# Two attention layers and their dense stages on one core: first tiles loaded a stage ahead, four row copies instead of eight, and a planned order with new costs

## The chip, the cores and the metric

The kernel runs on one core of one Trainium2 chip. The metric is device microseconds from start to end of one execution. The core has five instruction queues: TensorE (PE), VectorE (DVE), ScalarE (ACT), GpSimd (POOL) and SyncE (SP), which here only issues DMAs. Each takes its instructions strictly in the order in which they were written; they meet through semaphores.

## The reference, cut to what matters

```python
x = x + attn_a(layernorm(x))     # 2 x 2048 tokens, 256 wide, 16 heads of 16, causal
x = x + ffn(layernorm(x))        # 256 -> 1024 -> 256, gelu, weights replaced by alpha * sign(w)
x = x + attn_b(layernorm(x))     # biases, output projection, layernorm of its own with gamma, beta
x = x + ffn(layernorm(x))        # the same weights

def attn_a(x):
    q, k, v = heads(x @ W_attn)
    att = softmax(where(causal, q @ k.T / 4, -inf))
    att = att * decay            # after the softmax: falls with the distance, 0 from 511 tokens on
    return merge(att @ v) @ W_proj
```

All is float32. attn_b is the same without the decay, with biases and a normalisation behind its projection.

## The kernel before, in words

Six stages follow one another with a barrier of all engines between them; each has tiles and semaphores of its own, and tensors go from stage to stage through DRAM. They are `setup` (signs of the feed-forward weights), `projections` ("qkv_a": normalise x, q, k and v), `attention` ("att_a"), `dense` ("mid": output projection, residual, feed-forward, then q, k and v of the second attention), `attention` ("att_b") and `dense` ("end").

**Attention.** Tokens go in chunks of 512 (c = 0 to 3), heads in groups of 4; with two sequences that makes 8 groups (g = 0 to 7). A group's work has two halves. *Maxima* ("M"): PE multiplies 128 queries by up to 512 keys (line 982) and VectorE reduces that to the rows' negative maxima (lines 910 and 914); there are 160 a group, 1280 in all, and chunk c holds (c + 1) tenths of a group's. *Scores* ("S" and "X"): for a block of 128 keys against the 512 queries of a chunk, PE multiplies k by q (line 995) and subtracts the maxima's row by a matmul with a row of ones (line 1002), ScalarE takes the exponential (line 870), GpSimd multiplies by the decay in att_a (line 842) or clears the upper triangle in att_b (line 852), and PE multiplies by v (lines 1021 and 1030) and in att_a by ones for the sum (line 1016, "PO"; the product with v is "PV"). In att_a only the last two chunks of keys carry a decay that isn't 0; of the ones before ("far") only the exponentials' sums are needed, and ScalarE takes them from the maxima's own products (line 876).

Between maxima and scores of a chunk lies the item "MC": VectorE transposes the maxima (line 951), SyncE copies them by eight DMAs into `mx`, the row that line 1002 reads (line 808), and the first score of the chunk waits for these (semaphore `m_in`). "O" copies the finished output from PSUM (line 890) and SyncE stores it and copies the sums (lines 816, 818); "SU" takes their reciprocals (VectorE, lines 959 and 961; SyncE line 823 stores them to `inverse`). "L" is a load of k and q of one of four row sets r of a chunk of the next group; `FE`, `FM` and `FT` are the small steps for the far sums (lines 926 to 946).

**What sets the order.** The class `Plan` keeps a clock for each engine with written costs, and at each step takes the candidate that can start first, with a handicap: `URGENT` favours the second half of an open score, `PATIENCE` favours or delays a product by how many blocks of scores wait, `AHEAD` caps how far the maxima lead the scores (in groups), `APART` how far the two halves of PE rows drift apart. `ROW` is the assumed time from the transposed maxima to a usable row, `SUMS` from a copied output to its reciprocals. All five queues then run this one list in order. So an instruction whose input comes later than planned holds up all that is queued behind it on its engine. The last group takes its chunks in the order 3, 2, 1, 0. The loads of group g + 1 are placed from 6 us after the first score of group g, one of 16 each 2.8 us; the maxima of group g + 1's last chunk are planned from 56 us on.

**Starts.** At an attention stage's start SyncE issues all 32 loads of k of group 0 (line 762), then v (line 778, four), and waits; ScalarE's queue issues the 32 loads of q. At a dense stage's start SyncE loads y and inverse of chunk 0 (lines 1191, 1192), the vectors bo, gamma, beta (line 1204, last stage), then chunk 1 and x, then in the middle stage the q, k, v weights (line 1209); ScalarE's queue loads wp, x and the two sign matrices of 1 MB (lines 1401 to 1404). VectorE multiplies y by inverse (line 1481), PE projects (line 1336), VectorE adds the residual or bo (1495, 1489).

**Dense** runs 8 chunks of 512 tokens in an order written out by hand (`dense_plan`).

## Time and profile before

| | us |
|---|---|
| runs, not profiled | 2624.24 and 2630.41, median 2627.32 |
| profiled execution | 2634.41 |
| its span, first to last instruction | 2632.7 |
| PE / VectorE / ScalarE / GpSimd busy | 2354.9 / 1933.3 / 1470.5 / 1025.8 |
| PE's mean granted clock | 0.939 of full speed |

The times of the stages, lines and waits come from the one profiled execution. Times inside it count from its first instruction. Busy time of PE is modelled and two halves of the array can work at once, so a busy PE is not at its peak. A DMA row of SyncE is the time in which its queue issued it, not the transfer. The bracket at the end of a row is the idle time of the engine before it and what ended it.

### The profile page before, as it was taken

What the parts mean: (1) busy time and instruction counts of PE and PEld (TensorE: products, weight loads), DVE (VectorE), ACT (ScalarE), POOL (GpSimd) and SP (SyncE); (2) the same over time, 40 slices, a digit from 0 to 9 for tenths busy, and PEclk for the clock granted to TensorE, in tenths of its full rate; (3) what the DMA queues carried; (4) which work ended last, traced back from release to release, by engine and by line L of the source; (5) the groups of instructions that cost most, each with busy time, mean ns of one, the idle gap of its engine ahead of it and who ended that gap; (6) DMA issues with size and microseconds to landing.
All of it is one profiled execution on the core that took longest, in us unless ns stands there. A gap on an engine that the chain in (4) does not pass through costs nothing. (4 is left out here: it accounts for less than half of the span.)

```text
span 2632.7 us, 49993 instructions
## 1 busy us (share of the span) xinstructions
PE 2354.9 (89%) x16288; PEld 1350.9 (51%) x16288; DVE 1933.3 (73%) x4826; ACT 1470.5 (56%) x3293; POOL 1025.8 (39%) x1269
## 2 busy tenths in 40 slices
PE   4969999999989999939997599999999999992887
PEld 2534554555545555427774355554554544542666
DVE  5648888888888888417663499998888885913886
ACT  1217585776858687513332156767777777770333
POOL 0036787888787876921221100110110110013552
PEclk8969998999999999969998689999999999996999
DMA  4662031221303120053422620312212213004211
GB/s 153 260 136 70 16 76 32 60 58 39 86 10 82 36 57 10 10 155 105 145 97 97 121 74 6 87 45 52 72 38 74 58 35 90 6 14 142 88 40 33
DMA packets 165490, 188.72 MB, mean 72 GB/s; under 512 B 72944, under 2 KB 96240, under 8 KB 164464
## 3 DMA queue, kind: packets, MB, share of 16 engines
q1 hardware_dynamic: 159984, 175.55, 22.9%
q10 hardware_dynamic: 5248, 9.97, 1.8%
q8 instruction: 134, 2.20, 0.4%
q14 instruction: 124, 1.02, 0.1%
HBM read 114.37 MB, written 69.99 MB: 70 GB/s over the span
## 5 line engine op out<-in xcount | busy, mean ns | idle before, releaser
L842 POOL TENSOR_TENSOR att_a_wd<-att_a_wt,decay 128x256 f32<-128x256 f32 (+3 forms) x896 | 753.0, 876 | 225.5 <-ACT att_a_wt L870 214.6
L870 ACT ACTIVATE att_b_wt<-att_b_ps 128x512 f32<-128x512 f32 (+3 forms) x1280 | 588.7, 541 | 282.9 <-PE att_b_ps L1002 279.6
L910 DVE TENSOR_REDUCE att_a_mpart<-att_a_pm 128x1 f32<-128x512 f32 x768 | 494.4, 682 | 71.3 <-PE att_a_pm L982 70.2
L910 DVE TENSOR_REDUCE att_b_mpart<-att_b_pm 128x1 f32<-128x512 f32 x768 | 493.6, 683 | 69.3 <-PE att_b_pm L982 67.0
L870 ACT ACTIVATE att_a_wt<-att_a_ps 128x512 f32<-128x512 f32 (+3 forms) x896 | 408.1, 514 | 181.8 <-PE att_a_ps L1002 179.3
L995 PE MATMUL att_b_ps<-att_b_qop,att_b_kop 64*128 64x512 f32 (+3 forms) x1280 | 433.9, 410 | 14.9 <-DMA att_b_mx<-att_b_mrow 10.7
L982 PE MATMUL att_b_pm<-att_b_kop,att_b_qop 64*128 64x512 f32 (+3 forms) x1280 | 412.5, 422 | 22.1 <-DMA att_b_kop<-qk 19.2
L982 PE MATMUL att_a_pm<-att_a_kop,att_a_qop 64*128 64x512 f32 (+3 forms) x1280 | 358.2, 446 | 46.2 <-DMA att_a_kop<-qk 18.4
L852 POOL TENSOR_SCALAR_AFFINE_SELECT att_b_wt<-att_b_wt 128x512 f32<-128x512 f32 x128 | 81.6, 637 | 815.1 <-ACT att_b_wt L870 815.1
L1002 PE MATMUL att_b_ps<-att_b_mx,ones_row 64*128 64x512 f32 (+3 forms) x1280 | 386.4, 368 | 0.0
L982 PEld LDWEIGHTS att_a_pm<-att_a_kop,att_a_qop 64*128 64x128 f32 x1280 | 171.8, 192 | 292.6 <-DVE att_a_mpart L910 141.7
L995 PEld LDWEIGHTS att_b_ps<-att_b_qop,att_b_kop 64*128 64x128 f32 x1280 | 205.2, 187 | 216.5 <-ACT att_b_wt L870 188.5
L914 DVE CUSTOM_DVE_ANT_0 att_a_pm<-att_a_pm,late 128x128 f32<-128x128 f32 (+3 forms) x512 | 247.2, 500 | 90.4 <-PE att_a_pm L982 88.5
L876 ACT ACTIVATE att_a_pm<-att_a_pm,att_a_mpart 128x512 f32<-128x512 f32 x384 | 255.9, 667 | 86.0 <-DVE att_a_mpart L910 83.8
L1030 PE MATMUL att_b_po<-att_b_wt,att_b_va 128*17 128x512 f32 (+3 forms) x2560 | 296.1, 534 | 0.9 <-POOL att_b_wt L852 0.9
L995 PE MATMUL att_a_ps<-att_a_qop,att_a_kop 64*128 64x512 f32 (+3 forms) x896 | 281.9, 390 | 11.9 <-DMA att_a_mx<-att_a_mrow 11.9
L1002 PE MATMUL att_a_ps<-att_a_mx,ones_row 64*128 64x512 f32 (+3 forms) x896 | 286.6, 400 | 0.0
L982 PEld LDWEIGHTS att_b_pm<-att_b_kop,att_b_qop 64*128 64x128 f32 x1280 | 211.8, 191 | 141.0 <-DVE att_b_mpart L910 63.0
L914 DVE CUSTOM_DVE_ANT_0 att_b_pm<-att_b_pm,late 128x128 f32<-128x128 f32 (+3 forms) x512 | 245.3, 502 | 41.4 <-PE att_b_pm L982 40.3
L1002 PEld LDWEIGHTS att_b_ps<-att_b_mx,ones_row 64*128 64x128 f32 x1280 | 217.1, 189 | 9.9
L1016 PE MATMUL att_a_po<-att_a_wt,ones_strip 128*32 128x512 f32 (+3 forms) x1792 | 201.4, 522 | 0.0
L995 PEld LDWEIGHTS att_a_ps<-att_a_qop,att_a_kop 64*128 64x128 f32 x896 | 147.7, 190 | 63.7 <-ACT att_a_wt L870 26.9
(167 smaller groups left out, 3019.6 us busy)
## 6 DMA issues: line engine op xcount, KB each, us to landing
att_a_kop<-qk SPq DMA_DIRECT2D x256, 64.0 KB, 2.9
att_b_kop<-qk SPq DMA_DIRECT2D x256, 64.0 KB, 2.8
att_a_qop<-qk SPq DMA_DIRECT2D x224, 64.0 KB, 2.9
att_b_qop<-qk SPq DMA_DIRECT2D x224, 64.0 KB, 2.8
qk<-qkv_a_qk_hi SPq DMA_DIRECT2D x8, 1024.0 KB, 4.0
qk<-qkv_a_qk_lo SPq DMA_DIRECT2D x8, 1024.0 KB, 5.9
y<-att_a_y SPq DMA_DIRECT2D x32, 256.0 KB, 2.2
qk<-mid_qk_hi SPq DMA_DIRECT2D x8, 1024.0 KB, 4.2
```

The source lines that it names most:

```text
L842: pool.tensor_tensor(wd[:, v % WD, h, a:z], wt[:, v % buffers, h, a:z], keep["decay"][:, u:u + z - a], ALU.mult).then_inc(w_decayed, 1)
L852: pool.affine_select(out=block, in_=block, compare_op=ALU.is_ge, fill=0.0, base=0, pattern=[[0, GH], [1, P]], channel_multiplier=-1).then_ ...
L870: act.activation(wt[:, v % buffers, h, a:CH], pe_[:, n % EBANKS, 0:CH - a], ACT.Exp)\
L876: act.activation(pm[:, n % MBANKS, :], pm[:, n % MBANKS, :], ACT.Exp, bias=mpart[:, g % 2, c, piece, u:u + 1], accum_out=fsum[:, g % 2, c, ...
L910: dve.tensor_reduce(mpart[:, g % 2, c, piece, u:u + 1], pm[:, n % MBANKS, 0:w], AX.X, ALU.max, negate=True).then_inc(m_reduced, 1)
L914: dve.tensor_tensor_reduce(out=pm[:, n % MBANKS, 0:w], in0=pm[:, n % MBANKS, 0:w], in1=keep["late"][:, CH - w:CH], scale=-1.0, scalar=-2 * ...
L982: mm = pe.matmul(pm[:, n % MBANKS, 0:w], qop[rows, par, c, j, qb * P:(qb + 1) * P], kop[rows, par, j, piece * CH:piece * CH + w], start=Tr ...
L995: pe.matmul(pe_[:, n % EBANKS, 0:CH - a], kop[rows, par, j, kb * P:(kb + 1) * P], qop[rows, par, c, j, a:CH], start=True, stop=False)
L1002: mm = pe.matmul(pe_[:, n % EBANKS, 0:CH - a], keep["ones_row"][rows, :], mx[rows, par, c, j, a:CH], start=False, stop=True)
L1016: pe.matmul(po[STRIP * j:STRIP * (j + 1), a:CH], keep["ones_strip"][:, :], wt[:, v % buffers, j, a:CH], start=first, stop=False)
L1030: mm = pe.matmul(po[STRIP * j:STRIP * j + VW, a:CH], va[:, par, kb, j, :], wt[:, v % buffers, j, a:CH], start=first, stop=last)
```

## The change

Four things are changed.

1. `k_first` and `q_first`, chunk 0 of group 0, become lasting tiles. The stage in front fills them by 16 DMAs on SyncE: the first projections before the store of their last chunk, the middle stage before it stores its last q and k. The attention stage then loads only chunk 1 at its start (8 DMAs of k on SyncE, 8 of q on ScalarE's queue), and chunks 2 and 3 of group 0 through "L" items. k and q are now one tile a chunk.
2. `y`, `inverse`, `x` (two chunks each) and `wp` of the dense stages become lasting tiles. The attention stage in front loads them by 11 DMAs on SyncE when the first chunk of group 6 has its reciprocals.
3. The maxima's rows go by four DMAs of 16 partitions into two rows each, instead of eight of 8 into one.
4. The plan has new costs and, for each kind of attention, its own handicaps. After a product its clock goes on from the product's columns and a fixed time to leave. "SU" is placed 16 us after its output instead of 9 (7 for the last one).

```diff
-SEEN, ROW, SUMS = 290.0, 6000.0, 9000.0
-URGENT, WEIGH, APART, AHEAD = 60.0, 0.0, 6, 0.75
-PATIENCE = (500.0, 0.0, -600.0, -2000.0)
+SEEN, ROW, SUMS, LAST_SUMS = 290.0, 6000.0, 16000.0, 7000.0
+STRIPS, ENTER, LEAVE = 1 / 0.6, 80.0, 129.0
+MAXIMUM, FAR, EXP = 75.0, 690.0, (60.0, 0.84)
+TUNED = {True: (0.0, 4, 0.48, (1900.0, 200.0, 200.0, 100.0), 0.0, True),
+         False: (30.0, 3, 0.51, (200.0, 0.0, 200.0, -600.0), 0.0, True)}
...
@@ projections, SyncE
                     if not last or c + 2 < NC:
                         load(b, c + 2)
+                    if last and c == NC - 1:
+                        sp.wait_ge(stored[0], STORE * (B * NC // 2))
+                        load_first_chunk(sp, keep, dram, first_in)
                     store(b, c)
...
@@ class Plan
+        self.urgent, self.apart, self.most, self.patience, self.weigh, self.closed_first = TUNED[decayed]
...
         for c in range(NC):
-            self.loaded[0, c] = 5000.0 * c
+            self.loaded[0, c] = 8000.0 * c
+            for r in range(PAIRS if c > 1 else 0):
+                self.soon(8000.0 * (c - 1) + 1600.0 * r, "L", 0, c, r)
...
-                self.act = max(self.act, time) + 790.0
+                self.act = max(self.act, time) + FAR
...
-                self.soon(self.act + SUMS, "SU", g, item[2])
+                self.soon(self.act + (LAST_SUMS if (g, item[2]) == (GROUPS - 1, 0) else SUMS), "SU", g, item[2])
...
     def run(self, a, start, columns):
+        self.strips = False
...
-        self.dve = max(self.dve, end) + 100.0 + w / 0.96
+        self.dve = max(self.dve, end) + MAXIMUM + w / 0.96
...
-        self.act = max(self.act, ready) + 170.0 + (CH - a) / 1.4
+        self.act = max(self.act, ready) + EXP[0] + (CH - a) * EXP[1]
...
-        self.issued = start
-        self.free = [start + 180.0 + columns * 8 / 2.4 / 2] * 2
+        self.strips, self.issued = True, start + columns * STRIPS
+        self.free = [self.issued + LEAVE] * 2
...
-            self.done[v] = self.free[0] + SEEN
+            self.done[v] = self.issued + SEEN
...
-        both = max(self.free) + 90.0
+        both = self.issued if self.strips else max(self.free) + ENTER
...
-            if (g, c) in self.loaded and ahead < AHEAD:
+            if (g, c) in self.loaded and ahead < self.most:
...
-        if self.open:
+        if self.open and self.closed_first:
             return
...
-            if kind == "PO" and not self.decayed or GH * (v + 1) > self.scores - 0 * len(self.open):
+            if kind == "PO" and not self.decayed or GH * (v + 1) > self.scores - len(self.open):
                 continue
...
+            if kind == "PO" and first and self.closed < v:
+                continue
...
+def load_pair(eng, dram, g, c, r, k_too, q_too, loaded):
+    src = dram["qk"].rearrange("b h q g (j d) t -> b g h q d j t", d=HD)[g // NG, g % NG]
+    for a in range(2):
+        rows, heads = slice(HALF * a + HD * r, HALF * a + HD * (r + 1)), slice(GH // 2 * a, GH // 2 * (a + 1))
+        for t, half in ((k_too, src[r % 2, 1]), (q_too, src[r // 2, 0])):
+            if t is not None:
+                eng.dma_start(t[rows, :, :].bitcast(F32), half[:, heads, c * CH:(c + 1) * CH]).then_inc(loaded, 16)
+
+def load_first_chunk(eng, keep, dram, loaded):
+    for r in range(PAIRS):
+        load_pair(eng, dram, 0, 0, r, keep["k_first"], keep["q_first"], loaded)
+
+def load_y(eng, y, inverse, dram, b, c, loaded):
+    rows = dram["y"][b].rearrange("g (j s) t -> (g j) s t", s=STRIP)
+    for k in range(KT):
+        heads = slice(k * H // KT, (k + 1) * H // KT)
+        eng.dma_start(y[:, k, :], rows[heads, 0:HD, c * CH:(c + 1) * CH]).then_inc(loaded, 16)
+        eng.dma_start(inverse[:, k, :], dram["inverse"][b, c, heads, :].unsqueeze(1).to_broadcast([H // KT, HD, CH]))\
+           .then_inc(loaded, 16)
+
+def load_next(eng, keep, dram, x_src, w, loaded):
+    eng.dma_start(keep["wp"][:, :, :], w.rearrange("(t p) n -> p t n", p=P)).then_inc(loaded, 16)
+    for c in range(2):
+        load_y(eng, keep["y"][c], keep["inverse"][c], dram, 0, c, loaded)
+        eng.dma_start(keep["x"][c][:, :, :], at(x_src, 0, c)).then_inc(loaded, 16)
...
@@ attention, SyncE
-            for c in range(NC):
-                for r in range(PAIRS):
-                    load(sp, 0, c, r, True, False)
+            sp.sem_inc(qk_in[0][0], QK_LOADS)
+            for r in range(PAIRS):
+                load(sp, 0, 1, r, True, False)
             load_v(0)
...
-                    for a in range(2):
-                        row = mx[HALF * a:HALF * a + 1, g % 2, c, :, :].bitcast(F32)
-                        row = row.rearrange("o j (t k i) -> o (j t) k i", t=TB, k=P // SQUARE)
-                        for k in range(P // SQUARE):
-                            units = slice(SQUARE * k + SQUARE // 2 * a, SQUARE * k + SQUARE // 2 * (a + 1), SPREAD)
-                            sp.dma_start(row[:, :, k, :], mrow[units, c, :].bitcast(F32)).then_inc(m_in[c], 16)
+                    row = mx[0:P:HALF, g % 2, c, :, :].bitcast(F32).rearrange("o j (t k i) -> o (j t) k i", t=TB, k=P // SQUARE)
+                    for k in range(P // SQUARE):
+                        sp.dma_start(row[:, :, k, :], mrow[SQUARE * k:SQUARE * (k + 1):SPREAD, c, :].bitcast(F32))\
+                          .then_inc(m_in[c], 16)
...
+                if item == ("SU", GROUPS - 2, 0):
+                    for i in range(2):
+                        sp.wait_ge(y_out[i], Y_DMAS * (NG * NC // 2 + 1))
+                        sp.wait_ge(s_out[i], 16 * (NG * NC // 2 + 1))
+                    load_next(sp, keep, dram, x_src, w, next_in)
+            sp.wait_ge(next_in, NEXT_LOADS)
...
@@ attention, ScalarE
-            for c in range(NC):
-                for r in range(PAIRS):
-                    load(act, 0, c, r, False, True)
             act.sem_inc(e_weights, EBANKS)
             act.sem_inc(f_done, MBANKS)
+            for r in range(PAIRS):
+                load(act, 0, 1, r, False, True)
...
@@ dense, SyncE
-            load_y(0)
+            for i in range(2):
+                sp.sem_inc(y_in[i], Y_LOADS)
+                sp.sem_inc(x_in[i], 16)
             if norm:
                 for t, src in zip((bo, gamma, beta), norm):
                     sp.dma_start(t[:, :], row_of(src).to_broadcast([P, D])).then_inc(norm_in, 16)
-            load_y(1)
-            load_x(1)
...
+                if item == ("Q", CHUNKS - 1, M - 1):
+                    sp.wait_ge(qk_out[0], STORE)
+                    load_first_chunk(sp, keep, dram, first_in)
                 if item == ("Q", G, M - 1):
...
@@ dense, ScalarE
-            act.dma_start(wp[:, :, :], w.rearrange("(t p) n -> p t n", p=P)).then_inc(w_in, 16)
-            act.dma_start(x[:, 0, :, :], at(x_src, 0, 0)).then_inc(x_in[0], 16)
             act.dma_start(w1s[:, :, :].bitcast(F32), dram["w1s"]).then_inc(signs_in, 16)
```

## Rows read from the trace of the kernel before

**Rows 1.** Busy time by stage: us, PE, PEld, DVE, ACT, POOL, PE clock, DMA.

```profile
145.00:1138.00 993.00, 930.33 (x7680) 504.84 (x7680) 775.00 (x1980) 670.32 (x1713) 760.21 (x904) 0.95 0.20 49
1138.00:1466.00 328.00, 269.84 (x1088) 195.53 (x1088) 178.77 (x402) 99.90 (x129) 63.83 (x99) 0.91 0.37 126
1466.00:2378.00 912.00, 873.27 (x6400) 448.45 (x6400) 720.24 (x1891) 602.65 (x1313) 88.77 (x136) 0.96 0.22 53
2378.00:2633.00 255.00, 182.24 (x768) 141.00 (x768) 180.66 (x344) 69.55 (x89) 109.85 (x113) 0.88 0.24 77
```

**Rows 2.** Timeline, start of the first attention: start, us, what, idle before.

```profile
145.63 15.35 SPq L762 DMA_DIRECT2D att_a_kop<-qk  x32
161.03 8.27 SPq L778 DMA_DIRECT2D att_a_va<-v  x4
...
169.42 9.93 SPq L808 DMA_DIRECT2D att_a_mx<-att_a_mrow  x8
...
156.32 0.30 DVE L914 CUSTOM_DVE_ANT_0 att_a_pm<-att_a_pm,late 128x128 f32<-128x128 f32 x1 [9.94 <-PE att_a_pm L982]
...
180.42 0.79 PE L995 MATMUL att_a_ps<-att_a_qop,att_a_kop 64*128 64x512 f32 x2 [6.35 <-DMA att_a_mx<-att_a_mrow]
```

**Rows 3.** Timeline, start of the second attention.

```profile
1478.03 0.30 DVE L914 CUSTOM_DVE_ANT_0 att_b_pm<-att_b_pm,late 128x128 f32<-128x128 f32 x1 [10.61 <-PE att_b_pm L982]
...
1504.15 0.80 PE L995 MATMUL att_b_ps<-att_b_qop,att_b_kop 64*128 64x512 f32 x2 [8.84 <-DMA att_b_mx<-att_b_mrow]
```

**Rows 4.** Timeline, starts of the middle and the last stage.

```profile
1138.88 0.64 SPq L1191 DMA_DIRECT2D mid_y<-y  x1
...
1157.28 1.23 DVE L1481 TENSOR_TENSOR mid_yt<-mid_y,mid_inverse 128x1024 f32<-128x1024 f32 x1 [21.36 <-DMA mid_inverse<-inverse]
...
2395.88 1.23 DVE L1481 TENSOR_TENSOR end_yt<-end_y,end_inverse 128x1024 f32<-128x1024 f32 x1 [20.67 <-DMA end_inverse<-inverse]
...
2396.89 2.42 POOL L1273 TENSOR_TENSOR end_xb<-end_x,end_beta 128x1024 f32<-128x1024 f32 x1 [18.28 <-DMA end_beta<-in_L_attn_b_beta]
```

**Rows 5.** Busy time in five stretches of the attention stages.

```profile
2066.00:2096.00 30.00, 29.90 (x244) 15.96 (x240) 27.90 (x80) 22.37 (x52) 3.82 (x6) 1.00 0.35 99
2189.00:2219.00 30.00, 29.56 (x200) 12.78 (x198) 1.40 (x5) 22.92 (x51) 2.00 (x4) 1.00 0.35 98
1083.00:1131.00 48.00, 44.18 (x444) 22.11 (x444) 1.57 (x7) 23.07 (x57) 47.62 (x60) 0.99 0.04 13
549.10:661.70 112.60, 111.50 (x964) 61.01 (x960) 95.05 (x247) 83.05 (x214) 94.16 (x113) 1.00 0.21 54
1852.80:1957.10 104.30, 103.93 (x803) 52.19 (x803) 90.78 (x237) 75.26 (x165) 10.23 (x17) 1.00 0.21 58
```

**Rows 6.** Timeline of SyncE, ends of the stages before attention.

```profile
130.37 0.33 SPq L283 DMA_DIRECT2D v<-qkv_a_vt  x1
136.41 0.36 SPq L281 DMA_DIRECT2D qk<-qkv_a_qk_hi  x1
...
1437.43 0.36 SPq L1223 DMA_DIRECT2D x<-mid_x  x1
1456.90 0.36 SPq L1228 DMA_DIRECT2D qk<-mid_qk_hi  x1
```

**Rows 7.** Timeline: a burst of row copies, three reduces, three exponentials.

```profile
345.43 5.47 SPq L808 DMA_DIRECT2D att_a_mx<-att_a_mrow  x8
...
412.60 1.89 DVE L910 TENSOR_REDUCE att_a_mpart<-att_a_pm 128x1 f32<-128x512 f32 x3 [0.40 <-PE att_a_pm L982]
...
2330.77 1.57 ACT L870 ACTIVATE att_b_wt<-att_b_ps 128x512 f32<-128x512 f32 x3 [1.00 <-PE att_b_ps L1002]
```

**Rows 8.** The add of line 959, and GpSimd beside one of them.

```profile
L959 DVE TENSOR_TENSOR att_a_scol<-att_a_scol,att_a_frow x16: 181/296/7919, 284.9 to 1098.2; 128x32 f32<-128x32 f32 x16
...
403.30 19.51 POOL L842 TENSOR_TENSOR att_a_wd<-att_a_wt,decay 128x256 f32<-128x256 f32 x19 [1.10 <-ACT att_a_wt L870]
...
415.01 7.84 DVE L959 TENSOR_TENSOR att_a_scol<-att_a_scol,att_a_frow 128x32 f32<-128x32 f32 x1
```

More of the change, by code:

```diff
@@ L250, in projections @@
         hi_ready, lo_ready, v_kept, vt_filled = sm("hi_ready"), sm("lo_ready"), sm("v_kept"), sm("vt_filled")
-        stored = [sm(f"stored{i}") for i in range(2)]
+        stored, first_in = [sm(f"stored{i}") for i in range(2)], sm("first_in")
         block = ctx.enter_context(nc.Block())
@@ L634, in candidates @@
             first = kb == near(c, self.decayed)[0]
+            if kind == "PO" and first and self.closed < v:
+                continue
             start = max(both, self.issued, ready[v], self.kept if first and (kind == "PO" or not self.decayed) else 0.0)
             waiting = self.scores // GH - v
-            yield start, start + PATIENCE[max(0, min(waiting, len(PATIENCE)) - 1)], self.product, \
+            yield start, start + self.patience[max(0, min(waiting, len(self.patience)) - 1)], self.product, \
                 (kind, v, (z if kind == "PV" and self.decayed else CH) - a)
@@ L675, in attention @@
         sm = phase_semaphores(nc, ctx, name)
-        kop = sb("kop", [P, 2, GH // 2, T], F32R)
-        qop = sb("qop", [P, 2, NC, GH // 2, CH], F32R)
+        others = [(par, c) for par in range(2) for c in range(NC)][1:]
+        kop = {(0, 0): keep["k_first"], **{x: sb(f"kop{x[0]}{x[1]}", [P, GH // 2, CH], F32R) for x in others}}
+        qop = {(0, 0): keep["q_first"], **{x: sb(f"qop{x[0]}{x[1]}", [P, GH // 2, CH], F32R) for x in others}}
         mx = sb("mx", [P, 2, NC, GH // 2, CH], F32R)
@@ L791, in _ @@
                     load(sp, g, c, r, True, True)
-                    if (c, r) == (NC - 1, PAIRS - 1):
+                    if g and (c, r) == (NC - 1, PAIRS - 1):
                         if g > 1:
@@ L1112, in dense_plan, with dense @@
     return plan
-def dense(nc, name, x_src, x_dst, w, norm, weights, biases, keep, dram):
+def dense(nc, name, x_src, x_dst, norm, weights, biases, keep, dram):
     with ExitStack() as ctx:
@@ L1183, in _, with load_y_of @@
         def _(sp):
[L1184 to L1185 removed]
+            def load_y_of(G):
                 if G >= 2:
                     sp.wait_ge(yt_ready, G - 1)
[L1188 to L1194 removed]
+                load_y(sp, y[G % 2], inverse[G % 2], dram, G // NC, G % NC, y_in[G % 2])
             def load_x(G):
@@ L1581, in build @@
             "b1": sb("b1", [P, HT], F32), "b2": sb("b2", [P, KT], F32),
+            "k_first": sb("k_first", [P, GH // 2, CH], F32R), "q_first": sb("q_first", [P, GH // 2, CH], F32R),
+            "y": [sb(f"y_ahead{i}", [P, KT, CH], F32) for i in range(2)],
+            "inverse": [sb(f"inverse_ahead{i}", [P, KT, CH], F32) for i in range(2)],
+            "x": [sb(f"x_ahead{i}", [P, TB, D], F32) for i in range(2)],
+            "wp": sb("wp", [P, KT, D], F32),
         }
@@ L1585, in build @@
         projections(nc, "qkv_a", x[0], [(t["L0_attn_a_W_attn"], (0, 3 * D))], None, False, keep, scratch)
-        attention(nc, "att_a", True, keep, scratch)
-        dense(nc, "mid", x[0], x[1], t["L0_attn_a_W_proj"], None,
+        attention(nc, "att_a", True, x[0], t["L0_attn_a_W_proj"], keep, scratch)
+        dense(nc, "mid", x[0], x[1], None,
               [(t[f"L0_attn_b_W{n}"], (i * D, (i + 1) * D)) for i, n in enumerate("qkv")],
               [t[f"L0_attn_b_b{n}"] for n in "qkv"], keep, scratch)
-        attention(nc, "att_b", False, keep, scratch)
-        dense(nc, "end", x[1], x[2], t["L0_attn_b_Wo"], [t[f"L0_attn_b_{n}"] for n in ("bo", "gamma", "beta")],
+        attention(nc, "att_b", False, x[1], t["L0_attn_b_Wo"], keep, scratch)
+        dense(nc, "end", x[1], x[2], [t[f"L0_attn_b_{n}"] for n in ("bo", "gamma", "beta")],
               None, None, keep, scratch)
```

73 lines of the change are left out of this document (28 added, 45 removed).

## The prediction, as it went on record

> **What bounds the kernel now.** The page's chain of waits ends at the barrier that opens the last stage, so it says nothing of the four before it. I read each stage by its own windows, and then each stage's first microseconds in the timeline. [Rows 1] give the two attention stages 1905 of 2632.7 us, with VectorE busy 1495 of them; the reader should see no engine but PE near full there, and PE's busy share is modelled. The small stages hold 583 us after the first projections. Three kinds of lost time follow.
>
> First, every stage begins empty. In the first attention [rows 2] SyncE issues 32 loads of k (15.35 us), the loads of v, and only then the eight copies of the maxima's rows (9.93 us, against 5.47 us for the same eight later [rows 7]: the queue is full of bulk loads). VectorE idles 9.94 us before its first maximum at 156.32; PE idles 6.35 us before the first score at 180.42, 35 us after the stage's first load. In the second [rows 3] the same takes 10.61 and 8.84 us, and the first score comes at 1504.15, 37 us in. In the dense stages [rows 4] the first product of y and inverse waits for its loads from 1138.88 to 1157.28, and from the stage's start at about 2378 to 2395.88.
>
> Second, the steady groups. An attention group of the first stage takes 112.6 us with VectorE at 95 and GpSimd at 94; one of the second takes 104.3 us with VectorE at 90.8 [rows 5]. In the second stage the rate of exponentials is the same with maxima running beside them (52 in 30 us, VectorE 27.9 busy) as in a stretch with none (51 in 30 us, VectorE 1.4) [rows 5]. So scores, exponentials and products set its pace, not VectorE; the 30 us hole costs little by itself. The first stage's last 48 us hold 47.6 us of GpSimd [rows 5]: its tail is the decays.
>
> Third, two adds of one row copy, which take 0.296 us in the median, took over 7.8 us [rows 8].
>
> **The change, part by part.**
>
> *First k and q ahead.* The 32+32 loads at a stage's start become 8 on SyncE and 8 on ScalarE, for chunk 1; 16 go out in the stage in front, chunks 2 and 3 through the planned order. At (15.35/32) 0.48 us each the 16 take 7.7 us of SyncE. In the first projections they stand between the store of v at 130.37 and that of qk at 136.41 [rows 6]: 1.7 us late, while the last store, of v, is bound by VectorE; I cost it 0 (up to 2). In the middle stage SyncE is idle from 1437.43 to 1456.90 [rows 6]: 0. The first maximum then comes about 1 us after the barrier, saving 9 and 10 us. The first score needs chunk 0's 16 maxima (6 us at 0.60 us per 512 columns and 320 columns in the mean [rows 7]), and SyncE's 8 loads (3.9), v (1.9 at a load's price, 8.27 as now [rows 2]) and four row copies (2.7 to 5) with their landing, about 1. That puts it 11 to 19 us into the stage instead of 35 and 37. Group 0 is paced by VectorE, which recovers the 10 us in front and nearly all of the stall before the first score (6.4 and 8.8 us on PE), but new blocking of some 2 us arises where the plan places the score earlier than its row lands. I take **-17 us in each attention stage**, bounds -8 (only half the first idle) and -22 (all of the score's advance).
>
> *y, inverse, x and wp ahead.* Middle: 1157.28 moves to about 1139.2, **-18**. End: 2395.88 moves to about 2379, -17, but the three vectors of bo, gamma and beta are now what z waits for: beta was only used at 2396.89 behind everything [rows 4]; they are issued first and PE's product runs meanwhile, so I take 2 us of delay: **-15**, bounds -8 and -17. Late next could be the sign weights, issued on ScalarE's queue at the same moment; but the first hidden layer stands behind projection, normalisation and transposes, and far fewer bulk loads share the queue's engines with them: 0. What is added is 11 DMAs in group 6 of each attention stage, some 6 us of SyncE (13 if the queue fills, as it did from 1138.88 on). Queued behind them are the loads of group 7 and the rows of group 6; group 7's maxima in the second stage start right after their last load, so I charge **+1** each, bounds 0 and +8.
>
> *Four row copies instead of eight.* 5.47 us become about 2.7 [rows 7] if one of twice the rows costs the same to issue, and remain 5.5 if it costs twice. The stage's later scores wait little for rows: **-1 per attention stage**, bounds +1 and -4.
>
> *The planned order.* Its costs move onto the trace: a maximum was 633 ns and is 608, where three reduces take 1.89 us, a start-to-start of 0.60 [rows 7]; an exponential of 512 goes from 536 to 490, where three take 1.57 us, 0.485 [rows 7]. The lead of the maxima is capped at 0.48 and 0.51 of a group instead of 0.75, and products in the first stage are held back (500, 0, -600, -2000 become 1900, 200, 200, 100). No row shows an order that doesn't run yet. In the first stage 112.6 - 95.05 = 17.6 us a group lie open over VectorE; a sixth of it over 7 groups is 20 us, which I take because the plan had costed VectorE 5% and exponentials 9% too long: **-20**, bounds -70 (10 a group) and +60. In the second stage scores pace it at 104.3 us and nothing idles on PE: **-10**, bounds -35 and +45.
>
> *The reciprocals' place.* SUMS goes from 9 to 16 us, so that VectorE should not wait for a row copy. But the add at 415.01 took 7.84 us and ended at 422.85, just as GpSimd's unbroken run of 19 multiplies from 403.30 ended at 422.81 [rows 8]. The add reads two SBUF tiles, and it ended with that run, not with a landing. So I take **0**, bounds -15 and, below, a loss. The Trainium skill, "SBUF — State Buffer", section "Who interferes with whom", says that a VectorE instruction with two SBUF inputs contends with a GpSimd instruction that reads SBUF, and that the later one blocks fully; the trace agrees. If that rule holds, the later place changes nothing by itself; if the wait were for the copy, both stalls would go and the sum would be 15 us lower.
>
> The sum: -34 -33 +2 -2 -30 + 0 = **-97 us**. The profiled execution took 2634.41 us (span 2632.7), so 2537; it stands 7 us above the median of the runs shown, so **2530 us**, 3.7% less.
>
> **The rivals.**
>
> *The order gives much more.* Groups of the first stage fall to 103 us, 8 above VectorE's 95: 7 x 9.6 = 67 us; the second stage gives 3.5 a group, 24. With the 67 of the loads: 2634 - 67 - 91 = 2476, about 2469. For it: the open 17.6 us and the corrected costs. Against: PE shows no idle in the second stage.
>
> *The change doesn't do what it says.* The chunk is there but the score still waits, for v, the next chunk's loads and the rows on one queue, and the order gives nothing. Then the attention starts give 8 each and the dense stages 33, -49: 2578. With full starts and no order gain it is 2560.
>
> *The order costs some.* The cap lets rows come late: the last chunk holds 0.4 of a group's maxima, so in the second stage a lead of 0.51 leaves 0.11 x 104 = 11 us for transpose, copy and landing. A stall of 4 us in each of 14 groups is 56 in place of the order's 30 of gain: 2530 + 86 = 2616.
>
> *Slower: VectorE blocked behind GpSimd.* Held-back products and an earlier start let GpSimd run in unbroken backlogs, as in its 19.5 us run and in the tail [rows 5, 8]. The first stage has 16 such adds and 24 subtractions, also of two SBUF tiles. Two blocked for 7.8 us before. It decides when more than about 17 of these 40 block that long beyond the idle that VectorE has: 17 x 7.5 = 127 us cancel the loads' 67 and add 2% of loss. 25 would give 2634 - 67 + 25 x 7.5 = 2754, about 2747. Against it: the median of the 16 is 0.296 us though GpSimd is busy 94 of 112.6 us [rows 5, 8]. The skill's rule named above is this mechanism.
>
> **How the numbers follow.** Two per cent is about what a measurement of this kernel can tell from no change: 2574.8 and 2679.9. Forecast 0.47 (2490 to 2560); more from the order 0.17; the load part alone or half of it 0.17, of which 0.13 lies below 2574.8; the order costs some 0.14; slower by over 2% 0.05. So faster 0.77, same 0.18, slower 0.05. The range leaves out half of the small tail on the low side, the slow case and the worse part of the costly order: 2455 to 2600.
>
> **What would show it.** Right: first maxima about 1 us and first scores 11 to 19 us after the attention stages' barriers; the first product of y within 1 us of the dense stages' start; bursts of four row copies near 2.7 us; groups near 109 and 103 us. Wrong: a gap before the first score above 10 us; z waiting for bo in the last stage; group periods above 113 or 105 us; more adds over 5 us beside unbroken GpSimd runs; PE waiting for row copies at the last chunk of groups.

## The result, and the profile after

The changed kernel takes 2590.69 us (median of 2584.95 and 2596.43) against 2627.32 us; the ratio is 0.9859, interval 0.9812 to 0.9905. So it is 1.4% faster, where 3.7% was forecast. The profiled execution took 2584.95 us (span 2583.2), 49.5 us less than the one of before.

The first fence gives the busy time by stage of the changed kernel, in the columns of [rows 1].

```profile
150.00:1122.00 972.00, 928.34 (x7680) 513.99 (x7680) 776.88 (x1980) 670.97 (x1713) 754.09 (x904) 0.94 0.20 52
1122.00:1429.70 307.70, 268.52 (x1088) 194.63 (x1088) 178.66 (x402) 99.78 (x129) 63.63 (x99) 0.94 0.37 127
1429.70:2339.00 909.30, 877.02 (x6400) 444.32 (x6400) 721.48 (x1891) 602.48 (x1313) 88.42 (x136) 0.96 0.23 56
2339.00:2583.00 244.00, 188.06 (x768) 145.23 (x768) 180.16 (x344) 69.46 (x89) 109.52 (x113) 0.88 0.21 67
```

The busy times have hardly moved; the idle times have. From the start of one stage to the start of the next, in us (the first attention starts at 145.2 before and at 150.2 after):

| | before | after | measured | forecast |
|---|---|---|---|---|
| projections, to the first attention | 145.2 | 150.2 | +5.0 | 0 |
| first attention | 993.7 | 972.1 | -21.6 | -37 |
| middle | 327.5 | 307.6 | -19.9 | -18 |
| second attention | 912.1 | 909.3 | -2.8 | -27 |
| end | 254.2 | 244.0 | -10.2 | -15 |

(The forecast of an attention is its start, load_next, row copies and order together: -17 +1 -1 -20 and -17 +1 -1 -10.)

The starts came as forecast. In the timeline of the changed kernel the first maximum answers to [rows 2] and [rows 3], and the first product of y to [rows 4]:

```profile
151.26 0.69 PE L1025 MATMUL att_a_pm<-k_first,q_first 64*128 64x128 f32 x4 [11.45 <-SPq L820]
151.89 0.30 DVE L957 CUSTOM_DVE_ANT_0 att_a_pm<-att_a_pm,late 128x128 f32<-128x128 f32 x1 [0.45 <-PE att_a_pm L1025]
...
1122.38 1.23 DVE L1516 TENSOR_TENSOR mid_yt<-y_ahead,inverse_ahead 128x1024 f32<-128x1024 f32 x1 [2.98 <-SPq L1236]
...
1431.42 0.30 DVE L957 CUSTOM_DVE_ANT_0 att_b_pm<-att_b_pm,late 128x128 f32<-128x128 f32 x1 [0.51 <-PE att_b_pm L1025]
...
1466.88 2.25 SPq L845 DMA_DIRECT2D att_b_mx<-att_b_mrow  x4
1470.23 0.80 PE L1038 MATMUL att_b_ps<-att_b_qop,k_first 64*128 64x512 f32 x2 [5.49 <-DMA att_b_mx<-att_b_mrow]
...
2339.28 1.23 DVE L1516 TENSOR_TENSOR end_yt<-y_ahead,inverse_ahead 128x1024 f32<-128x1024 f32 x1 [3.96 <-SPq L1236]
2339.50 0.34 SPq L1240 DMA_DIRECT2D end_bo<-in_L_attn_b_bo  x1
...
2349.49 1.23 DVE L1524 TENSOR_TENSOR end_z<-end_pp,end_bo 128x1024 f32<-128x1024 f32 x1 [8.98 <-DMA end_beta<-in_L_attn_b_beta]
```

VectorE's first maximum stands 2 us behind each attention's start, and TensorE's first scores come 15 and 14 us behind it, against 35 and 38 before. One stall for a row is left, 5.49 us at the second chunk. In the end stage z waits for the norm vectors, as feared, but for 9 us behind their issue, not for 2.

The loss is in the last two groups of each attention. Waits of TensorE in the changed kernel, first from 870 to 990 us, then from 2100 to 2200 us (engine, line, awaited: us in total, times, longest):

```profile
PE att_a_pm L1025 <- DMA att_a_qop<-qk: 15.4, 1, 15.4
```

```profile
PE att_b_pm L1025 <- DMA att_b_qop<-qk: 9.7, 1, 9.7
```

Both are the first maximum of group 7, waiting for that group's k and q. SyncE's timeline in front of the second shows what stands before those loads:

```profile
2134.59 0.71 SPq L711 DMA_DIRECT2D wp<-in_L_attn_b_Wo  x1
2135.34 0.64 SPq L704 DMA_DIRECT2D y_ahead<-y  x1
...
2141.83 1.26 SPq L714 DMA_DIRECT2D x_ahead<-x  x1
2143.13 2.52 SPq L690 DMA_DIRECT2D att_b_kop<-qk  x1
2145.69 0.42 SPq L690 DMA_DIRECT2D att_b_qop<-qk  x1
```

These are load_next's eleven DMAs, 8.5 us of SyncE with 3.3 MB. The stretches behind them, with TensorE's stall; the last three columns are the granted clock, the share of the DMA engines and GB/s:

```profile
2134.00:2150.00 16.00, 16.00 (x112) 8.55 (x108) 15.02 (x32) 12.70 (x26) 0.00 (x0) 1.00 0.67 187
2150.00:2170.00 20.00, 11.38 (x81) 4.32 (x80) 3.66 (x10) 7.68 (x17) 1.27 (x2) 0.89 0.97 157
2170.00:2180.00 10.00, 8.93 (x51) 5.79 (x51) 5.92 (x13) 3.15 (x9) 1.27 (x2) 0.53 0.07 14
```

The DMA engines are 0.97 busy while TensorE has 11.4 us of work in 20, and afterwards its granted clock is 0.53 over 10 us, close to the lower of its two levels (1.2 GHz), so part of the stall is paid for twice: once as idle time, and once more as slower matmuls behind it.

### The profile page after: what moved, and what is told of

It reads as the page before. It is cut to its first block and busy times, and to the rows that moved or that the text cites. A ratio compares the mean times of both kernels' runs of the same rounds, so it can differ in the third digit from the quotient of the medians.

```text
span 2583.2 us, 49748 instructions
## 1 busy us (share of the span) xinstructions
PE 2362.2 (91%) x16288; PEld 1360.0 (53%) x16288; DVE 1936.0 (75%) x4826; ACT 1470.7 (57%) x3293; POOL 1018.8 (39%) x1269
## 5 line engine op out<-in xcount | busy, mean ns | idle before, releaser
L1045 PE MATMUL att_b_ps<-att_b_mx,ones_row 64*128 64x512 f32 (+3 forms) x1280 | 401.0, 370 | 0.0
L1025 PE MATMUL att_a_pm<-att_a_kop,att_a_qop 64*128 64x512 f32 (+3 forms) x1024 | 337.6, 426 | 31.4 <-DMA att_a_qop<-qk 15.4
L1025 PE MATMUL att_b_pm<-att_b_kop,att_b_qop 64*128 64x512 f32 (+3 forms) x1024 | 355.7, 408 | 11.3 <-DMA att_b_qop<-qk 9.7
L1038 PE MATMUL att_b_ps<-att_b_qop,att_b_kop 64*128 64x512 f32 (+3 forms) x1024 | 357.0, 410 | 2.4 <-ACT att_b_wt L913 0.9
L1045 PE MATMUL att_a_ps<-att_a_mx,ones_row 64*128 64x512 f32 (+3 forms) x896 | 306.0, 403 | 0.0
L1038 PEld LDWEIGHTS att_b_ps<-att_b_qop,att_b_kop 64*128 64x128 f32 x1024 | 166.1, 185 | 203.9 <-ACT att_b_wt L913 193.5
L1038 PE MATMUL att_a_ps<-att_a_qop,att_a_kop 64*128 64x512 f32 (+3 forms) x768 | 264.6, 397 | 0.0
L1045 PEld LDWEIGHTS att_b_ps<-att_b_mx,ones_row 64*128 64x128 f32 x1280 | 226.0, 191 | 9.0
L1025 PEld LDWEIGHTS att_b_pm<-att_b_kop,att_b_qop 64*128 64x128 f32 x1024 | 178.4, 190 | 85.9 <-DVE att_b_mpart L953 47.2
L1038 PEld LDWEIGHTS att_a_ps<-att_a_qop,att_a_kop 64*128 64x128 f32 x768 | 129.6, 187 | 86.6 <-ACT att_a_wt L913 50.8
```

What stands on the lines that cost most here:

```text
L1025: mm = pe.matmul(pm[:, n % MBANKS, 0:w], qop[par, c][rows, j, qb * P:(qb + 1) * P], kop[par, piece][rows, j, 0:w], start=True, stop=True)
L1038: pe.matmul(pe_[:, n % EBANKS, 0:CH - a], kop[par, kb // TB][rows, j, kb % TB * P:(kb % TB + 1) * P], qop[par, c][rows, j, a:CH], start=Tr ...
L1045: mm = pe.matmul(pe_[:, n % EBANKS, 0:CH - a], keep["ones_row"][rows, :], mx[rows, par, c, j, a:CH], start=False, stop=True)
```

## The experiments

Twelve kernels ran. Each ratio is to the kernel before, timed in the same job. Stage lengths come from one profile each, and run from the start of a stage to the start of the next (the 952 and 891 that expectations name for both moves are 955.3 and 895.0 so measured). "The late versions" are the kernels with the new order, four row copies and load_next late: six for the first attention, and for the second the three of them that leave it otherwise alone.

### load_next one group later

```diff
-                if item == ("SU", GROUPS - 2, 0):
+                if item == ("MC", GROUPS - 1, 0):
```

> The changed kernel, but the 11 loads for the dense stage behind (y, inverse, x, wp) are issued after the last row copy of group 7 instead of after the first reciprocals of group 6. Theory 1 (they stand in SyncE's queue and on the DMA engines in front of group 7's k and q, and PE waits 15.4 and 9.7 us for these): both waits shrink below 3 us, the second attention's group 6 falls from 121 us to about 104, the stages shorten by 10 to 15 us each, and the kernel takes about 2565 us, 25 less than the changed one. Theory 2 (the new order itself holds group 6 up, and the loads are late only because of it): the waits stay above 8 us and the time moves by less than 8 us. A third outcome would be that the loads, now later, hold up the dense stages' start: the first product of y then comes over 5 us after the barrier.

2553.44 us, ratio 0.9716 (0.9676 to 0.9756). The first attention takes 950.7 instead of 972.1, the second 894.9 instead of 909.3. TensorE's two waits are gone. Theory 1 holds and was too small: 10 to 15 us a stage and 25 in all were expected. The DMA issues from 2134 to 2170 us of the changed kernel, and of the same stretch of work (2115 to 2150 us) of this one (KB each, median us from issue to landing):

```profile
att_b_kop<-qk SPq DMA_DIRECT2D x14, 64.0 KB, 8.4
att_b_qop<-qk SPq DMA_DIRECT2D x14, 64.0 KB, 8.7
att_b_va<-v SPq DMA_DIRECT2D x4, 136.0 KB, 6.6
```

```profile
att_b_qop<-qk SPq DMA_DIRECT2D x15, 64.0 KB, 3.2
att_b_kop<-qk SPq DMA_DIRECT2D x14, 64.0 KB, 3.1
att_b_va<-v SPq DMA_DIRECT2D x4, 136.0 KB, 3.4
```

The same loads land in 3.1 us instead of 8.4. This one line brings as much again as the whole change did, 37 us. That is its price under the new order; what it is under the old one comes below.

### The two halves of the change

*loads_only* keeps the planner's old costs and handicaps in the changed kernel:

```diff
...
-TUNED = {True: (0.0, 4, 0.48, (1900.0, 200.0, 200.0, 100.0), 0.0, True),
-         False: (30.0, 3, 0.51, (200.0, 0.0, 200.0, -600.0), 0.0, True)}
...
+URGENT, WEIGH, APART, AHEAD = 60.0, 0.0, 6, 0.75
+PATIENCE = (500.0, 0.0, -600.0, -2000.0)
...
```

> The changed kernel with the order's costs and handicaps of before (633 ns a maximum, lead 0.75, products as before, reciprocals after 9 us); the loads ahead and the four row copies stay. Theory 1 (the loads give some 60 us less what they cost group 7, the new order some 20 in the first attention and nothing in the second): about 2600 us, the first attention about 20 us longer than in the changed kernel, groups of 113 us there, the second attention within 6 us of it, 909. Theory 2 (the new order costs time in the second attention): the second attention is shorter than 900 us, and the kernel takes 2580 us or less.

*order_only* puts the new planner alone into the kernel before.

> The kernel before with the new order alone: new costs and handicaps, all loads as before, eight row copies. Theory 1 (the order gives about 20 us in the first attention, nothing in the second): about 2608 us, the second attention 908 to 915 us with groups of 104, no wait of PE for group 7's k and q over 5 us. Theory 2 (the order costs in the second attention): over 920 us there, and 2627 or more in all.

loads_only took 2581.12 us, ratio 0.9819 (0.9782 to 0.9857); order_only 2631.12 us, 1.0015 (0.9987 to 1.0042). The new order alone gives nothing, and within the changed kernel the old one does no worse. Read no further, this would say that the order is worthless. By stage it is two effects: alone it shortens the first attention from 993.7 to 982.7 and lengthens the second from 912.1 to 929.1. Within the changed kernel, where load_next is early, it lengthens both: 961.5 with the old order and 972.1 with the new one, then 903.0 and 909.3. order_only bears out its theory 2, the order's cost in the second attention. loads_only fits neither of its theories: the one had the first attention 20 us longer under the old order, the other had the second under 900.

### Half of the first loads one chunk earlier

```diff
-                    if last and c == NC - 1:
-                        sp.wait_ge(stored[0], STORE * (B * NC // 2))
-                        load_first_chunk(sp, keep, dram, first_in)
+                    if last and c >= NC - 2:
+                        if c == NC - 2:
+                            sp.wait_ge(stored[0], STORE * (B * NC // 2 - 1))
+                        for r in (0, 1) if c == NC - 2 else (2, 3):
+                            load_pair(sp, dram, 0, 0, r, keep["k_first"], keep["q_first"], first_in)
```

> As next_late, and of the 16 loads of the first k and q 8 are issued one chunk earlier in the first projections, so that SyncE is free when the last q and k are to be stored. Theory 1 (the changed kernel's projections end 5 us late because the last 2 MB of q and k are stored 4 us late behind the 16 loads): the first attention starts at 145 to 146 us instead of 150.2, and the kernel takes 4 to 5 us less than next_late, about 2560. The rival (the loads' traffic itself holds up the stores): it starts at 149 to 150 and nothing is gained.

2545.41 us, ratio 0.9675 (0.9638 to 0.9712), on top of the later load_next. In the changed kernel the sixteen loads end right ahead of the last stores:

```profile
139.80 0.42 SPq L690 DMA_DIRECT2D q_first<-qk  x1
...
140.27 0.42 SPq L286 DMA_DIRECT2D qk<-qkv_a_qk_hi  x1
140.74 0.51 SPq L286 DMA_DIRECT2D qk<-qkv_a_qk_lo  x1
141.29 1.10 SPq L288 DMA_DIRECT2D v<-qkv_a_vt  x1
```

The store that stood at 136.41 [rows 6] is at 140.27, and the barrier waits for the landing of all three. With the loads split the first attention starts at 146.6 instead of 150.7 (145.7 to 147.6 in the other kernels that split them). "Both moves" below means this kernel; the rest builds on it.

### Does TensorE set the steady groups?

```diff
-                                       wt[:, v % buffers, j, a:CH], start=first, stop=last)
+                                       wt[:, v % buffers, j, a:z], start=first, stop=last)
```

(with z = CH where the block is first or on the diagonal, else CH // 2, on both operands; half of the output of the other blocks is left out)

> The same two moves with the new order; in the second attention the value product of the 21 blocks per group that are neither a chunk's first nor on its diagonal runs over half its columns (that part of the output is left out). It takes 21 x 256 columns at 1.67 ns, 9 us, of TensorE out of each group. Theory 1 (TensorE sets the steady groups' 104 us): period 95 to 97, the second attention 820 to 835 instead of 891. Theory 2 (VectorE, busy 90 of 104, with its chain of maximum, row, score sets it): period 102 to 104, the attention over 875.

2485.08 us in its one run; the second attention's stage falls from 895.0 to 829.5. A steady group of the changed kernel (first stage, then second), and one of this kernel's second stage:

```profile
561.00:671.00 110.00, 108.83 (x961) 59.42 (x960) 95.55 (x248) 83.25 (x215) 93.34 (x112) 1.00 0.21 55
1790.00:1894.00 104.00, 103.81 (x800) 52.02 (x800) 89.78 (x237) 74.73 (x163) 10.15 (x16) 1.00 0.22 58
```

```profile
1739.00:1834.00 95.00, 94.80 (x800) 51.73 (x798) 89.03 (x236) 74.80 (x164) 10.20 (x16) 1.00 0.29 64
```

Nine microseconds of TensorE taken out shorten the group by nine, with the same 800 matmuls and VectorE unchanged. In the second attention TensorE is the bound, and [rows 5] already said so: 103.93 busy of 104.30. An order can fill no gap there.

### Order and row copies, two by two

*old_best* is both moves with the old planner (the diff of loads_only).

> The changed kernel with load_next one group later and half of the first loads one chunk earlier (the run before took 2545.4 us), but the planner with its old costs and handicaps. Theory 1 (TensorE is full in the steady groups of the second attention, 103.8 of 104 us, so that no order can shorten them, and the order matters only where an attention starts and ends): the second attention stays within 6 us of 891, and the whole within 8 us of 2545. Theory 2 (the planned order is worth what was forecast once load_next no longer eats it): 2575, that is 30 us above, some 20 of them in the first attention.

*best_eight* is both moves with eight row copies instead of four:

```diff
+                    for a in range(2):
+                        row = mx[HALF * a:HALF * a + 1, g % 2, c, :, :].bitcast(F32)
...
+                            units = slice(SQUARE * k + SQUARE // 2 * a, SQUARE * k + SQUARE // 2 * (a + 1), SPREAD)
```

> The same two moves with the new order, but the row maxima copied by eight DMAs of four rows instead of four of eight. Theory 1 (a copy's length counts only where a score waits for it, at the start of each attention: about 5.5 us against 2.5): 2 to 6 us above 2545. Theory 2 (SyncE's queue is what delays the loads, and twice the copies, 32 more per group, push them back in every group): over 10 us above, with TensorE waiting for the last loads of group 7 again.

*old_eight* has both, the old planner and eight copies.

> Both moves with the old order, and the row maxima by eight DMAs. With the new order eight copies cost 21 us in the second attention (911 against 890), TensorE waiting 1.5 us for a row in every group. Theory 1 (only the new order puts the first score of a chunk so close behind its last maximum that a copy's length is waited for; the old one keeps 0.75 of a group between them): 2 to 5 us above the four-copy version with the old order (2570), both of it at the attentions' starts. Theory 2 (eight copies cost every group, whatever the order): 15 to 25 us above.

| | us | ratio | interval | attention 1 | attention 2 |
|---|---|---|---|---|---|
| old order, eight copies | 2578.58 | 0.9831 | 0.9804 to 0.9858 | 980.8 | 900.3 |
| new order, eight copies | 2575.82 | 0.9776 | 0.9738 to 0.9814 | 963.8 | 915.1 |
| old order, four copies | 2570.05 | 0.9771 | 0.9728 to 0.9813 | 972.7 | 891.8 |
| new order, four copies (both moves) | 2545.41 | 0.9675 | 0.9638 to 0.9712 | 955.3 | 895.0 |

The new order is worth 17 us in the first attention with either kind of copy, as these profiles have it. In the second it loses 15 with eight copies and 3 with four. So old_best refutes neither theory whole: the second attention is where theory 1 put it, the first where theory 2 did. But the 17 us can't all be laid to the order. Up to group 6 old_best and loads_only run the same attention, and yet old_best's first attention reaches the first exponential of group 6 727.8 us in, and loads_only's 713.8. That spread of 14 us is nearly as large as the gain; the late versions stand at 711.8 to 726.2. From that exponential to the stage's end the order shows more clearly: 244.8 us with the old one, 233.5 to 239.3 (mean 237.2) with the new one. The timed ratios, over several executions each, bear a gain out only with four copies and load_next late: 0.9771 to 0.9675, intervals apart, or some 25 us. With eight copies the intervals touch (0.9831 to 0.9776), and with load_next early there is none (loads_only 0.9819, the changed kernel 0.9859).

Why eight copies hurt under the new order shows in TensorE's waits over the second attention, with eight copies, and then with four (the kernel of the next section, which differs in nothing else in that stage):

```profile
PE att_b_ps L1042 <- DMA att_b_mx<-att_b_mrow: 19.5, 9, 9.2
```

```profile
PE att_b_ps L1040 <- DMA att_b_mx<-att_b_mrow: 5.5, 1, 5.5
```

A burst of eight still takes 5.47 us, one of four 2.25. The lead of 0.51 of a group leaves the score too close behind its row for the long burst: nine waits, where the short one leaves only the start's. With the old order the eight copies cost 8 us in each stage, 16.6 in all. That is the size of theory 2 (15 to 25) and not of theory 1 (2 to 5), but not theory 2's reason: in the second attention the steady groups are as long as with four copies, and the cost is the start (from the stage's start to group 1's first exponential 164.2 us instead of 155.5). In the first attention the start is worth 2.4 us (156.3 and 153.9), and the rest is no larger than the spread above.

### Sign weights behind the norm vectors

```diff
+            if norm:
+                act.wait_ge(norm_in, N_NORM)
             act.dma_start(w1s[:, :, :].bitcast(F32), dram["w1s"]).then_inc(signs_in, 16)
```

> The same two moves with the new order, and ScalarE issues the two sign loads (1 MB each) of the mid and end stages only once the three norm vectors have landed. Theory 1 (at the end stage's start beta's 9 us landing, beside the 2 MB of sign weights, holds GpSimd and with it z): z starts some 5 us earlier in the end stage, mid gains 0 to 3, the whole is 4 to 8 us below 2545. Theory 2 (the signs are then late for the first sign matmul, about 22 us into the stage): the same or up to 5 us above.

2550.64 us, ratio 0.9679 (0.9639 to 0.9719): as a whole no different from both moves, where 4 to 8 us had been expected. The condition leaves the middle stage as it was, so that the 0 to 3 us named for it had no edit behind them. In the end stage beta's landing frees z earlier:

```profile
2308.46 1.23 DVE L1520 TENSOR_TENSOR end_yt<-y_ahead,inverse_ahead 128x1024 f32<-128x1024 f32 x1 [3.98 <-SPq L1238]
...
2314.02 0.35 ACTq L1442 DMA_DIRECT2D end_w_signs<-w1s  x1
...
2315.68 1.23 DVE L1528 TENSOR_TENSOR end_z<-end_pp,end_bo 128x1024 f32<-128x1024 f32 x1 [5.99 <-PE end_pp L1375]
```

z stands 7.2 us behind the first product instead of 10.2, and now waits for TensorE. The stage takes 238.7 us, and 238.0 in *mix*, against 240.4 to 244.1 in the other kernels with early y.

### Queue or bytes?

*next_small* issues load_next at its old place, each DMA with a part of its columns (an eighth of y and inverse, a quarter of x and wp, 0.6 MB of the 3.3 in all), and the full ones a group later. *next_pool* issues the full ones at the old place in the second attention, but from GpSimd.

```diff
                 if item == ("SU", GROUPS - 2, 0):
...
+                    load_next_eighth(sp, keep, dram, x_src, w, next_in)
...
```

```diff
+                if not decayed and item == ("SU", GROUPS - 2, 0):
...
+                    load_next(pool, keep, dram, x_src, w, next_in)
```

> The new order with both moves, but load_next's eleven DMAs are also issued at their old place (group 6's last inverses), each with an eighth of its columns; the full ones follow one group later. So SyncE's queue has the eleven issues, and the DMA engines an eighth of the bytes. Theory 1 (the place in SyncE's queue delays group 7's loads): the first attention 10 to 15 us and the second 10 to 14 us above both_moves' 952 and 891, TensorE again waiting 8 us or more ahead of group 7. Theory 2 (the 3.3 MB on the DMA engines delay them): both within 3 us. Half and half: some 6 us of TensorE's wait in each.

> The new order with both moves in the first attention; in the second, load_next goes back to its old place, but GpSimd, which is idle there, issues it. So SyncE's queue is free of it, and the DMA engines carry all its bytes beside group 7's loads. Theory 1 (queue): the second attention at 891 (within 3). Theory 2 (bytes): 900 to 906, TensorE waiting some 5 to 10 us ahead of group 7.

next_small: 2556.53 us, ratio 0.9751 (0.9729 to 0.9774); the second attention takes 894.4 us against 895.0, the first 961.0 against 955.3. The eleven issues fill 6.5 us of SyncE and delay nobody in the second. Nor do they in the first: from group 6's first exponential on it takes 238.0 us, within the 233.5 to 239.3 of the late versions, and its extra lies before the eleven issues. next_pool: 2564.05 us, 0.9793 (0.9760 to 0.9826); the second attention takes 902.1, and TensorE waits again:

```profile
PE att_b_pm L1032 <- DMA att_b_qop<-qk: 4.7, 1, 4.7
```

The place in SyncE's queue, which I had priced, costs nothing; the bytes cost 7.5 us from a queue of their own, as theory 2 had it, and 14.7 (909.3 against a mean of 894.6 of the three versions with load_next late) when they also stand ahead of group 7's loads in the same one. That the second half comes from that order is argued, not shown.

### The new order in the first attention, the old one in the second

```diff
-    return Plan(decayed, mbanks, ebanks, buffers, wd).make()
+    return (Plan if decayed else OldPlan)(decayed, mbanks, ebanks, buffers, wd).make()
```

(with both moves, and the sign weights behind the norm vectors)

> Both moves, the sign loads behind the norm vectors, the new order in the first attention and the old one in the second. Theory 1 (the new order gains some 10 to 17 us in the first attention, and loses 2 to 3 in the second, where TensorE is full in either): the second attention at 888, the whole at 2541, 2 to 4 us below the version with the new order in both. Theory 2 (the two orders differ by nothing in the second attention): the same as that.

2545.36 us, ratio 0.9710 (0.9689 to 0.9731), span 2540.6, the shortest profile of a kernel that leaves nothing out. The second attention takes 891.0 against 893.8, the 3 us expected. The median is that of both moves, taken in another job; the timing doesn't tell the two apart, and gives no sign of the 3 us. By their ratios either beats the changed kernel (0.9859) by 1.5 to 1.9%, and the one before by about 3%.

## Why the prediction was wrong

In the order of its terms; the attention stages' lengths can be walked from before to after through kernels that ran:

| | attention 1 | attention 2 | forecast |
|---|---|---|---|
| loads ahead, load_next late (before to old_eight) | -12.9 | -11.8 | -17 each |
| four row copies (old_eight to old_best) | -8.1 | -8.5 | -1 each |
| new order (old_best to the late versions) | -16.4 | +2.8 | -20, -10 |
| load_next early (late versions to after) | +15.8 | +14.7 | +1 each |
| sum | -21.6 | -2.8 | -37, -27 |

The late versions are the means of six profiles with identical code in the first attention (956.3, from 950.7 to 959.7) and of three in the second (894.6, from 893.8 to 895.0). So a step in the second attention is good to 1 or 2 us. In the first, a step between two kernels of the new order is good to some 4 us, and one that begins or ends at a kernel of the old order to no better than 14, the spread of old_best and loads_only up to group 6.

The steps also depend on the way that is walked, since order and load_next meet. Attention 1, then attention 2:

| | old order | new order |
|---|---|---|
| load_next late | 972.7, 891.8 (old_best) | 956.3, 894.6 (late versions) |
| load_next early | 961.5, 903.0 (loads_only) | 972.1, 909.3 (the changed kernel) |

Through loads_only the new order would read +10.6 and +6.3 instead of -16.4 and +2.8. The stretch from group 6's first exponential to the stage's end holds load_next, and is freer of what came before: there load_next early costs 3.0 and 12.3 us under the old order, and 11.8 and 15.4 under the new one. The timed ratios have the same shape: 0.9771 to 0.9819 under the old order (a part of it the split first loads), and 0.9716 to 0.9859 under the new one without that part.

**load_next is the step that failed.** The prediction charged "+1 each, bounds 0 and +8", having seen that "queued behind them are the loads of group 7". It measured +15.8 and +14.7 (+11.8 and +15.4 if only the stretch from group 6 on is laid to it): of the 39.6 us by which the attentions missed, some 25 to 28.5. I had counted the eleven issues as time of SyncE, and next_small shows that this time is free; the 3.3 MB that they bring were never divided by what the DMA engines carry. [Rows 5] showed those engines only 0.21 busy over a group, a mean over a group whose loads come in its first half. In the first attention the cover had also been cut by the other half of the change: with late loads, group 7's first maximum stands 60 to 65 us behind group 6's first score under the new order, and 74 us under the old. With load_next early the two come 78 and 83 us behind, the one with 15.4 us of idle TensorE, the other with 5.7. In the second attention the orders hardly differ (59 and 56 us), and TensorE waits 9.7 us for group 7's q under the new one and 8.8 under the old.

**The order's term was right in one attention at most.** -20 became -16.4 in the first, as a difference of profiles that hold the spread above, and only with load_next late; the timed ratios give 25 us there for the kernel as a whole. With load_next early, as the change has it, nothing of it shows. The first attention's steady groups fell from 112.4 us to some 110.2, where 109 had been forecast. In the second -10 became +2.8, though the prediction had noted that "nothing idles on PE" there: a group of 104 us stayed at 104. The 10 us should have been 0 by its own rows. The rival in which a cap of 0.51 lets rows come late is real in the second attention, +15 us, but only where the rows go by eight copies. The two parts hide each other's price.

**The row copies were under-sized,** 8.5 us for 1 in the second attention, since I priced the burst and not who waits for it while a start's loads fill the same queue. In the first attention the 8.1 us aren't told from the spread. The burst itself was right: 2.25 against the forecast of 2.7.

**The starts.** First maxima and first scores came where they were put, but gave 12 and 13 us an attention instead of 17 (the first again with the old order's spread). The sum of starts and row copies, 41, is near the 36 of the forecast, by two errors that cancel; that is luck.

**The dense stages.** Middle -19.9 for -18. End -10.2 for -15: beta landed 9 us behind its issue, beside 2 MB of sign weights; the order of those loads gives back 3 us at z. The first loads in front of the first attention cost 5 us, above the bound of 2, since the stores behind them ended that stage.

**The reciprocals' place, 0: nothing speaks against it, and no run changes it alone.** The adds of [rows 8], line 1002 in the changed kernel:

```profile
L1002 DVE TENSOR_TENSOR att_a_scol<-att_a_scol,att_a_frow x16: 181/738/7469, 301.4 to 1082.6; 128x32 f32<-128x32 f32 x16
```

The longest is 7.5 us after 7.9; they sum to 25.8 us after 23.3. But with the old place loads_only has a sum of 10.0, and none over 1.5 us, and old_best one of 40.9, so that the place alone doesn't decide it. That an add waits for GpSimd's run of multiplies, as the prediction read it, shows again in old_best:

```profile
1074.17 33.29 POOL L882 TENSOR_TENSOR att_a_wd<-att_a_wt,decay 128x384 f32<-128x384 f32 x38
1082.18 25.33 DVE L998 TENSOR_TENSOR att_a_scol<-att_a_scol,att_a_frow 128x32 f32<-128x32 f32 x1 [22.00 <-DMA att_a_scol<-att_a_y]
```

The run ends at 1107.46 and the add at 1107.51. Such waits are a likely part of the old order's spread: old_best has one of 6.7 us in group 1, which takes 120.0 us, and loads_only has none there and takes 110.5. The slower rival, with seventeen or more of them, never came: no profile has more than two adds over 5 us.

What stays open: what the order is worth in the first attention to better than this, for which each kernel of the old order would need several profiles; how load_next's bytes and their place ahead of group 7's loads share its price there (next_pool leaves the first attention alone); and whether another lead than 0.48 would serve an early load_next.

## What to carry to other kernels

A prefetch has two prices, the issue time on its queue and its bytes on the DMA engines; look in the windows just behind its place for loads that somebody needs soon, and put it where there are none, here one group later. Where an engine is busy for the whole of a steady period, no order shortens it, so plan only its edges. And when parts of a change meet on one resource, price them together: in the second attention shorter row copies were worth 20.5 us under an order that keeps little lead and 8.5 under the old one, and in the first the same order brought group 7's first maximum some 12 us closer, so that an early load_next cost more.

## What the hardware showed that I had not expected

A single k or q load took SyncE 2.52 us to issue, and in the first attention 3.83, right behind load_next, against 0.42 otherwise; four loads of v took 7.2 us against 2.6. The engines then moved only 157 GB/s at 0.97 busy, while the mix with y and x just before moved 187 at 0.67. A row copy of 16 partitions costs the queue no more than one of 8: four of the larger take 2.25 us, eight of the smaller 5.47. And a stall of 9.7 us on TensorE was followed by 10 us at a granted clock of 0.53.
